# Adaptive layer norm, linear attention and a routed expert layer on one core: weight maxima turned later, norm shifts joined, one turning transfer per tile, filling matmuls in idle stretches

## The chip, the cores and the metric

One Trainium2 chip, of which the kernel uses 1 core. The metric is the time of one execution on the device in microseconds (us). The profile comes from one execution with the hardware profiler on; its span runs from the first to the last recorded instruction.

## What is computed

Input x is 16 batches of 256 tokens with 128 features. A modulation table of shape 16 x 6 x 128, from a small product, gives shifts, scales and gates. Cut to what matters:

```python
h = _layernorm(x) * (1 + ca) + sa
x = x + ga * attention(h)      # relu features, running sums of k v^T, 16 heads of 8
h = _layernorm(x) * (1 + cb) + sb
x = x + gb * ffn(h)
# ffn:
h = rmsnorm(s @ W_in.T, in_norm_w)
logits = h @ Wr.T              # 8 experts, the best 2 of each token, softmax over the two
gate = silu(h @ Wg[e].T); up = h @ Wu[e].T       # 128 -> 512
oe = rmsnorm(gate * up @ Wd[e].T, enorm_w[e])    # 512 -> 128
out = out + gates[:, e:e + 1] * oe
s_hat = rmsnorm(out, out_norm_w) @ W_out.T
```

Everything is fp32 to the outside. The expert weights and the dispatched rows are split in an fp16 high part and an fp16 low part, so that each expert product is three fp16 matmuls.

## The kernel before, in words

All five engines run programs written out by hand, with semaphores between them; nothing schedules. The kernel has three phases.

**Phase one, steps over the 16 batches.** `pipelined` calls `step` on every engine with six stages at once (nrm, qkv, att, prj, inp, rte), each one batch behind the one ahead of it. Steps 0 to 7 are written out, steps 8 to 15 are a hardware loop of two steps a turn, then comes one more step and `drain`, which finishes batches 12 to 15. On TensorE (PE) a step begins with `running_state(att, 0)`: three chunks of three matmuls each against a triangle, into the banks CUM[0] to CUM[2] (L1474). Chunk 0 and 1 come first, then the transposes of the two norms' outputs (L1516, L1525), then chunk 2, which also waits for `den_done`, the denominators of the batch before (VectorE, L1097). There follow the spreading of reciprocals (L1534), keys and values (L1551, L1554), queries (L1561), the output projection (L1578, L1581), `running_state(att, 1)`, the ranks of the chosen experts (L1595 to L1601), the router's input (L1611) and `head_sums` for both halves (L1492 to L1503). VectorE (DVE) makes den and its reciprocal at a step's start, `running_products(att, 0)`, routing and norms, `running_products(att, 1)`, and at the end `weights`. Activations, conversions and the turned copies hT, h2T are on ScalarE (ACT); k v products and the indirect scatters of the routed rows into the table `dispatched` are on GpSimd (POOL): four scatters a batch (L536).

**Weight maxima.** The fp16 split needs one power of two for all expert weights. In steps 3 to 6 `weights` reduces two pieces of the weights each to maxima per partition (L1056), and at the end of step 6 to one column, wmax (L1061, L1062). SCALE_STEP is 7. In that step PE turns wmax to a row (MAX_ROW, in the spare columns of bank CUM[1], L1466) ahead of chunk 1 of the first half, `weight_power` on DVE (L1075 to L1077) takes the power of two, PE broadcasts it to all partitions ahead of chunk 1 of the second half (MAX_ALL, L1469), and `weight_scale` on DVE (L1083 to L1086) makes the factors ahead of `running_products(att, 1)`. From step 8 on the loop converts one eighth of the weights a step.

**Norm shifts.** A norm's shift, minus mean times inverse deviation, is computed by `norm_shift` with one operation for each of the two token tiles of a batch (L883); in the drain the second norm's shift is one operation already (L1220).

**Between the phases.** In the drain PE alternates between `spread` (L1620), `turn` (L1629), `project` (L1636, L1639), `into_experts` (L1651) and `ranks` (L1664 to L1669), each waiting for ACT or DVE. Then PE sums the counts (TOTAL, L1700), DVE computes the tail positions and the table of tiles (39 tiles of 256 rows, each with its expert and first row), SP and ACT write filler rows behind each expert's rows in `dispatched`, and SP waits for all scatters, all fillers and the table, loads the table's first rows to registers (L447), and fetches tile by tile.

**Phase two, tiles.** `load_rows` on SP fetches a tile's high and low rows by two turning (transposing) transfers of 256 rows x 128 fp16 (L433), up to three tiles ahead. PE's `gate_up` runs 24 fp16 matmuls of 256 columns (L1723 to L1725) and `down` 24 of 128 (L1738 to L1740), with the weight's place taken from a register with the expert's number. ACT, DVE and POOL gate, split, weigh and scatter the results. **Phase three** loads the expert rows back, mixes, projects and stores.

## Time and profile before

| what | value |
|---|---|
| median of 3 runs | 413.69 us (413.61 to 415.18) |
| profiled execution, its own time | 414.08 us |
| its span | 412.2 us |
| PE busy | 354.4 us, 86%, 3757 matmuls |
| DVE busy | 323.8 us, 79% |
| ACT busy | 291.9 us, 71% |
| POOL busy | 236.5 us, 57% |
| chain that ended last | PE 70%, DVE 10%, ACT 6%, issue 5%, DMA 4% |
| granted TensorE clock, mean | 0.939 |

The profiled execution's own time is 1.9 us more than its span, which leaves out what lies around the first and last instruction. Phase one ends near 196 us, the tiles run from 209.9 to about 370 us, the rest is phase three. A matmul's shown duration includes the way through the array, so that gapless matmuls overlap in it; the distance of two starts is what one costs. The clock's 1.00 is 2.4 GHz, 0.50 is 1.2 GHz.

### The profile page before, as it was taken

To read this page: it belongs to the slowest core of one execution; us is meant where nothing else is said; L and a number is where in the kernel's file an instruction comes from. 1 tells how busy PE (TensorE), PEld (TensorE's weight loads), DVE (VectorE), ACT (ScalarE), POOL (GpSimd) and SP (SyncE) were. 2 spreads that over 40 slices of the span, in tenths; PEclk is the share of its full clock that TensorE was granted. 3 is DMA by queue.
4 is the path that set the end of the run, shared out by engine and by line. 5 is a ranking of instruction groups with operands and counts; after the bars stand their busy time and mean duration, and the time that the engine had idled before them with its cause. 6 is when DMAs were issued, how large, how long until landed. Compare 5 with 4: busy or idle time off the path is not lost.

```text
span 412.2 us, 12923 instructions
## 1 busy us (share of the span) xinstructions
PE 354.4 (86%) x3757; PEld 307.9 (75%) x3758; DVE 323.8 (79%) x1037; ACT 291.9 (71%) x814; POOL 236.5 (57%) x211
## 2 busy tenths in 40 slices
PE   7899998999999999982069999999999999990464
PEld 4788886888888888861049889989899898980443
DVE  5568998899999999976928887878778877870696
ACT  5465776888888888546328878778778787773595
POOL 0665585688888888856341645454454445453441
PEclk9999998999999999995559999999999999997698
DMA  7899000000000000111423333333333333213833
GB/s 217 356 368 363 2 28 26 8 30 27 26 26 26 26 26 26 34 40 51 131 40 54 68 71 70 62 71 60 64 64 71 60 69 65 57 34 110 351 94 94
DMA packets 46563, 35.68 MB, mean 87 GB/s; under 512 B 36291, under 2 KB 42070, under 8 KB 45750
## 3 DMA queue, kind: packets, MB, share of 16 engines
q1 hardware_dynamic: 41862, 25.40, 21.9%
q0 software_dynamic: 4544, 9.39, 7.0%
q10 hardware_dynamic: 128, 0.53, 0.5%
q8 instruction: 15, 0.25, 0.3%
q14 instruction: 14, 0.11, 0.1%
HBM read 18.69 MB, written 13.47 MB: 78 GB/s over the span
## 4 chain that ended last, share of the span: by engine, by line
PE 70%; DVE 10%; ACT 6%; issue 5%; DMA 4%; POOL 1%; SPq 1%; DVEq 0%; ACTq 0%; POOLq 0%
PE bank L1474 12%; PE bank L1723 9%; PE bank L1724 8%; PE bank L1725 8%; PE bank L1738 4%; PE bank L1740 4%; PE bank L1554 4%; PE bank L1739 4%; PE bank L1497 3%; DVE prod L960 2%; ACT junk L835 2%; DVE wmaxs L1056 1%; PE bank L1561 1%; DMA cst<-consts 1%; PE bank L1581 1%
## 5 line engine op out<-in xcount | busy, mean ns | idle before, releaser
L559 POOL DMA_INDIRECT expert_rows<-late,to_place x78 | 79.2, 1015 | 85.9 <-DVE late L1333 73.3
L1723 PE MATMUL bank<-late,w_hi 128*128 128x256 f16 x312 | 86.4, 277 | 15.1 <-DMA late<-dispatched 13.7
L1724 PE MATMUL bank<-late,w_hi 128*128 128x256 f16 x312 | 86.4, 277 | 0.0
L1725 PE MATMUL bank<-late,w_lo 128*128 128x256 f16 x312 | 86.3, 276 | 0.0
L518 POOL TENSOR_TENSOR kv<-kv,v 128x1024 f32<-128x1024 f32 x32 | 67.7, 2134 | 32.0 <-ACT kv L686 32.0
L1319 DVE SCALAR_TENSOR_TENSOR kv<-bank,uscale,kv 128x512 f32<-128x512 f32 x78 | 58.5, 750 | 30.4 <-ACT kv L777 18.6
L536 POOL DMA_INDIRECT dispatched<-rows,pos x64 | 67.3, 1051 | 25.7 <-issue 18.2
L1474 PE MATMUL bank<-cst,kv 128*128 128x128 f32 x576 | 74.3, 279 | 0.0
L777 ACT ACTIVATE kv<-bank,descale 128x512 f32<-128x512 f32 x78 | 53.6, 687 | 24.0 <-PE bank L1725 20.1
L1474 PEld LDWEIGHTS bank<-cst,kv 128*128 128x128 f32 x576 | 68.9, 193 | 0.3 <-issue 0.2
L783 ACT ACTIVATE kv<-kv 128x512 f16<-128x512 f32 x78 | 48.8, 625 | 16.8 <-DVE kv L1319 12.3
L1326 DVE TENSOR_TENSOR kv<-kv 128x512 f16<-128x512 f32 x78 | 54.4, 697 | 7.5 <-ACT kv L783 5.6
L1738 PE MATMUL bank<-late,kv 128*128 x312 | 54.3, 219 | 0.5 <-DVE kv L1326 0.5
L1739 PE MATMUL bank<-late,kv 128*128 x312 | 54.3, 219 | 0.0
L1740 PE MATMUL bank<-late,kv 128*128 x312 | 54.3, 219 | 0.0
L960 DVE TENSOR_TENSOR prod<-bank,qT 128x384 f32<-128x384 f32 x96 | 49.6, 544 | 0.2 <-issue 0.2
L1723 PEld LDWEIGHTS bank<-late,w_hi 128*128 x312 | 30.9, 99 | 20.5 <-issue 16.5
L1725 PEld LDWEIGHTS bank<-late,w_lo 128*128 x312 | 31.0, 99 | 4.0
L1724 PEld LDWEIGHTS bank<-late,w_hi 128*128 x312 | 31.0, 99 | 3.4
L1738 PEld LDWEIGHTS bank<-late,kv 128*128 128x128 f16 x312 | 30.5, 98 | 1.1 <-issue 0.6
L1739 PEld LDWEIGHTS bank<-late,kv 128*128 128x128 f16 x312 | 30.5, 98 | 0.4
L1740 PEld LDWEIGHTS bank<-late,kv 128*128 128x128 f16 x312 | 30.5, 98 | 0.0
(233 smaller groups left out, 733.2 us busy)
## 6 DMA issues: line engine op xcount, KB each, us to landing
late<-wguT SPq DMA_DIRECT2D x1, 4096.0 KB, 17.8
late<-expert_rows SPq DMA_DIRECT2D x1, 2064.0 KB, 10.9
gates_bc<-gate_rows SPq DMA_DIRECT2D x1, 2048.0 KB, 6.9
wd<-wdT SPq DMA_DIRECT2D x1, 2048.0 KB, 25.0
out<-kv SPq DMA_DIRECT2D x16, 128.0 KB, 1.8
late<-dispatched SPq DMA_TRANSPOSE x78
expert_rows<-late,to_place POOLq DMA_INDIRECT x78
late<-expert_rows SPq DMA_DIRECT2D x1, 1032.0 KB, 6.5
```

Source lines behind the costliest of these rows:

```text
L518: nc.gpsimd.tensor_tensor(kvt[:, 0:HD, :, :], k_in, v_in.to_broadcast([P, HD, H, HD]), ALU.mult).then_inc(kv_done[t], 1)
L536: pool.indirect_dma_start(hbuf, bass.IndirectOffsetOnAxis(ap=pos[:, p, t * K + k:t * K + k + 1], axis=0), rows[:, p, t, k, :], None).then_ ...
L559: pool.indirect_dma_start(ybuf, bass.IndirectOffsetOnAxis(ap=to_place[:, s, r:r + 1], axis=0), yt[:, s, r, :], None).then_inc(y_scat[s], 16)
L960: nc.vector.tensor_tensor(prod[:, t, cc * THIRD * P:(cc + 1) * THIRD * P].rearrange("p (e i) -> p e i", i=P), cum, qT[:, p, t * P:(t + 1) ...
L1319: nc.vector.scalar_tensor_tensor(gu[:, h, :], U[h], uscale[:], sg[:, h, :], ALU.mult, ALU.mult).then_inc(gu_done, 1)
L1474: last = mm(CUM[cc][:, j * P:(j + 1) * P], kv[:, p, t, e * D:(e + 1) * D], tri, start=True, stop=True)
L1723: mm(o, w_hi[:, w], hi, start=True, stop=False)
L1724: mm(o, w_hi[:, w], lo, start=False, stop=False)
L1725: last = mm(o, w_lo[:, w], hi, start=False, stop=True)
L1738: mm(o, gu_hi[:, s % 2, h, g], wd_hi[:, w], start=(f == 0 and r == 0), stop=False)
L1739: mm(o, gu_lo[:, s % 2, h, g], wd_hi[:, w], start=False, stop=False)
L1740: last = mm(o, gu_hi[:, s % 2, h, g], wd_lo[:, w], start=False, stop=(f == FC - 1 and r == RB - 1))
```

## The change

Six edits:

1. The turning of wmax moves from the first half of the scale step to the second (still ahead of chunk 1); the broadcast moves to the step's very end on PE, into spare columns of the bank FFN, behind waits for `wpow_done` and for the chosen slots. On DVE `weight_power` moves behind `running_products(att, 1)` and `weight_scale` to the end of the step, waiting for a new semaphore `wall_ps`.
2. `norm_shift` is one operation for both token tiles.
3. A tile's rows are fetched by one turning transfer of 256 rows x 256 fp16.
4. SP's waits for scatters and fillers move behind the register load.
5. PE's filling matmuls (`keep_busy`, bf16, 512 columns, results unused): 5, 13, 3 and 12 in the drain, 24 behind TOTAL, and 8 once the scatters have landed, ahead of the first tile.
6. The weights' places in the tile phase are formed as byte offsets.

```diff
-        MAX_ALL = CUM[1][:, THIRD * P:THIRD * P + 1]
+        MAX_ALL = FFN[:, L + NT * E:L + NT * E + 1]
...
-            sp.wait_ge(scattered[0], 16 * NT * K * (B // 2))
-            sp.wait_ge(scattered[1], 16 * NT * K * (B // 2))
-            sp.wait_ge(filled, 16 * (E + 1))
             sp.wait_ge(table_done, 1)
...
-                for half in range(2):
-                    sp.dma_start(hT3[:, s, half], hbuf16[bass.ds(row, R), half * D:(half + 1) * D],
-                                 transpose=True).then_inc(slot_ld[s], 16)
+                sp.dma_start(hT3[:, s], hbuf16[bass.ds(row, R), 0:2 * D], transpose=True).then_inc(slot_ld[s], 16)
...
                 sp.load(row_regs, tile_row[0:1, bass.ds(TURN * i, TURN)])
+                if not again_turn(i):
+                    sp.wait_ge(filled, 16 * (E + 1))
+                    sp.wait_ge(scattered[0], 16 * NT * K * (B // 2))
+                    sp.wait_ge(scattered[1], 16 * NT * K * (B // 2))
...
-                for t in range(NT):
-                    last = nc.vector.tensor_scalar(nmr_[:, p, t:t + 1], mv_[:, p, t, 0:1], -1.0, rs_[:, p, t:t + 1],
-                                                   ALU.mult, ALU.mult)
-                last.then_inc(nm_done, 1)
+                nc.vector.scalar_tensor_tensor(nmr_[:, p, :], mv_[:, p, :, 0], -1.0, rs_[:, p, :], ALU.mult,
+                                               ALU.mult).then_inc(nm_done, 1)
...
-                    if scale and cc == 1:
-                        if t == 0:
-                            pe.wait_ge(wmax_done, 1)
-                            mm(MAX_ROW, wmax[:], ident, start=True, stop=True)
-                        else:
-                            pe.wait_ge(wpow_done, 1)
-                            mm(MAX_ALL, ones[0:1, :], wpow_row[:], start=True, stop=True)
+                    if scale and t and cc == 1:
+                        pe.wait_ge(wmax_done, 1)
+                        mm(MAX_ROW, wmax[:], ident, start=True, stop=True)
...
+                if scale:
+
+                    pe.wait_ge(wpow_done, 1)
+                    pe.wait_ge(ohs_done, rte[0] + 1)
+                    mm(MAX_ALL, ones[0:1, :], wpow_row[:], start=True, stop=True).then_inc(wall_ps, 1)
+
+            def keep_busy(bank, n):
+                for _ in range(n):
+                    mm(bank[:].rearrange("p (a n) -> p a n", n=P), ones16[:],
+                       ones16[:].unsqueeze(1).to_broadcast([P, 4, P]), start=True, stop=True)
...
             mm(TOTAL, ones16[:], oh_all[:, B, NT * K, :], start=True, stop=True).then_inc(total_ps, 1)
+            keep_busy(CUM[0], 24)
...
+            def columns_of(w, e, per_expert, at):
+
+                return w.bitcast(U8)[:, bass.ds(e * (2 * per_expert) + 2 * at, 2 * P)].bitcast(F16)
...
             pe.wait_ge(moe_ld, 32)
+            pe.wait_ge(scattered[0], 16 * NT * K * (B // 2))
+            pe.wait_ge(scattered[1], 16 * NT * K * (B // 2))
+            keep_busy(CUM[0], 8)
             turn_of_tiles(0, first=True)
```

PE's program in the scale step, first half, as it stands before (x counts neighbours alike; `bank` is any PSUM bank):

```order
L1503 MATMUL bank<-s,qT 128x16
L1474 MATMUL bank<-cst,kv 128x128 x3
L1466 MATMUL bank<-cst,wmax 1x128
L1474 MATMUL bank<-cst,kv 128x128 x3
L1516 MATMUL bank<-cst,xn 128x128 x2
L1525 MATMUL bank<-cst,xn 128x128 x2
L1474 MATMUL bank<-cst,kv 128x128 x3
L1534 MATMUL bank<-cst,rden 128x128 x2
L1551 MATMUL bank<-bkv,ones 128x512
```

and of the change, the first rows of the step and its second half and end:

```order
L1466 MATMUL bank<-cst,kv 128x128 x6
L1508 MATMUL bank<-cst,xn 128x128 x2
L1517 MATMUL bank<-cst,xn 128x128 x2
L1466 MATMUL bank<-cst,kv 128x128 x3
...
L1466 MATMUL bank<-cst,kv 128x128 x3
L1461 MATMUL bank<-cst,wmax 1x128
L1466 MATMUL bank<-cst,kv 128x128 x6
...
L1495 MATMUL bank<-s,qT 128x16
L1612 MATMUL bank<-wpow_row,cst 128x1
```

The matmul that reads wmax stands behind the projection and chunk 0 of the second half, and the one that reads wpow_row is the last of the step.

DVE's program at the end of the scale step, of the change (before, the three rows of wmax_row and wpow_row stood behind `running_products(att, 0)`, and the four from wpow on ahead of the three `prod`):

```order
L958 TENSOR_TENSOR prod<-bank,qT 128x384 x3
L1073 TENSOR_REDUCE wmax_row<-bank 1x1
L1074 TENSOR_SCALAR wmax_row<-wmax_row 1x1
L1075 TENSOR_SCALAR wpow_row<-wmax_row 1x1
L878 RECIPROCAL rs<-sd 128x2
L998 TENSOR_TENSOR ohs<-oh_all,bank 128x32
L882 SCALAR_TENSOR_TENSOR nmr<-mv,rs 128x2
L1014 TENSOR_REDUCE pos<-ohs 128x4
L1005 TENSOR_REDUCE oh_all<-oh_all 128x8
L1081 COPY wpow<-bank 128x1
L1082 RECIPROCAL wscale<-wpow 128x1
L1083 TENSOR_SCALAR descale<-wpow 128x1
```

The factors' four operations (the fourth, w_by, follows) now stand right ahead of the next step's den.

PE's program at the end of the drain, of the change; before, the same rows stood there without those that read only `ones`:

```order
L1653 MATMUL bank<-small,h2T 128x136 x2
L1616 MATMUL bank<-ones 128x512 x13
L1666 MATMUL bank<-region,ones 128x16
L1668 MATMUL bank<-oh_all,strict 128x16 x2
L1669 MATMUL bank<-oh_all,ones 128x16
L1671 MATMUL bank<-oh_all,ones 128x8 x2
L1631 MATMUL bank<-cst,xn 128x128 x2
L1616 MATMUL bank<-ones 128x512 x3
L1653 MATMUL bank<-small,h2T 128x136 x2
L1616 MATMUL bank<-ones 128x512 x12
```

The fillers stand between `into_experts` and `ranks`, where PE waited for the one-hots, and between `turn` and `into_experts`, where it waited for h2T.

## Rows read from the trace of the kernel before

**Rows 1.** The page's TensorE clock, in 40 slices of the span.

```profile
PEclk9999998999999999995559999999999999997698
```

**Rows 2.** Busy time by stretch; the clock is granted share of 2.4 GHz.

```profile
64.80:68.60 3.80, 1.95 (x16) 1.56 (x16) 3.59 (x11) 1.72 (x6) 2.59 (x3) 1.00 0.11 35
68.70:72.00 3.30, 3.30 (x15) 2.53 (x14) 2.22 (x9) 1.91 (x6) 1.19 (x2) 0.50 0.12 40
181.00:184.70 3.70, 1.85 (x16) 1.34 (x17) 2.88 (x18) 2.78 (x8) 1.24 (x3) 1.00 0.11 36
...
201.30:205.60 4.30, 0.00 (x0) 0.00 (x0) 4.27 (x6) 2.68 (x3) 0.08 (x1) 0.50 0.54 169
...
209.90:215.40 5.50, 5.50 (x27) 3.88 (x28) 0.94 (x2) 1.89 (x3) 1.09 (x1) 0.50 0.27 51
...
390.00:409.90 19.90, 12.95 (x82) 9.72 (x82) 17.41 (x70) 17.01 (x79) 6.76 (x11) 1.00 0.31 90
```

**Rows 3.** PE timeline around the scale step: start, duration, engine, line, operation, idle before.

```profile
57.18 0.39 PE L1551 MATMUL bank<-bkv,ones 3*128 3x512 bf16 x1 [0.20 <-ACT hT L662]
...
64.77 0.92 PE L1474 MATMUL bank<-cst,kv 128*128 128x128 f32 x6
67.54 0.38 PE L1466 MATMUL bank<-cst,wmax 128*1 128x128 f32 x2 [1.85 <-DVE wmax L1062]
...
79.64 1.58 PE L1474 MATMUL bank<-cst,kv 128*128 128x128 f32 x12
```

**Rows 4.** DVE timeline of the same steps and, last row, of the drain.

```profile
54.96 0.18 DVE L1097 TENSOR_SCALAR den<-bank 128x32 f32<-128x32 f32 x1
...
67.50 0.18 DVE L1097 TENSOR_SCALAR den<-bank 128x32 f32<-128x32 f32 x1
...
74.13 0.32 DVE L883 TENSOR_SCALAR nmr<-mv,rs 128x1 f32<-128x1 f32 x2
...
75.92 0.16 DVE L1083 COPY wpow<-bank 128x1 f32<-128x1 f32 x1
...
76.63 1.48 DVE L960 TENSOR_TENSOR prod<-bank,qT 128x384 f32<-128x384 f32 x3
...
181.11 0.16 DVE L1220 SCALAR_TENSOR_TENSOR nmr<-mv,rs 128x2 f32<-128x2 f32 x1
```

**Rows 5.** PE timeline of the drain.

```profile
178.63 0.63 PE L1651 MATMUL bank<-small,h2T 128*128 128x136 f32 x4
...
182.27 0.44 PE L1620 MATMUL bank<-cst,rden 128*128 128x128 f32 x2 [1.44 <-ACT rden L618]
...
184.61 1.01 PE L1651 MATMUL bank<-small,h2T 128*128 128x136 f32 x4
188.55 0.19 PE L1664 MATMUL bank<-region,ones 1*128 1x16 bf16 x1 [2.93 <-DVE oh_all L994]
...
188.94 0.69 PE L1629 MATMUL bank<-cst,xn 128*128 128x128 f32 x2
190.28 1.27 PE L1651 MATMUL bank<-small,h2T 128*128 128x136 f32 x4 [0.66 <-ACT h2T L629]
194.79 0.19 PE L1664 MATMUL bank<-region,ones 1*128 1x16 bf16 x1 [3.24 <-DVE oh_all L994]
```

**Rows 6.** Chain that ended last, from the last scatter on: start, duration.

```profile
200.42 5.17 DMA dispatched<-rows,pos
...
205.66 0.32 SPq L447
...
206.10 1.21 SPq L433
...
207.46 2.28 DMA late<-dispatched
```

**Rows 7.** PE timeline, the first tile matmul.

```profile
209.87 0.39 PE L1723 MATMUL bank<-late,w_hi 128*128 128x256 f16 x1 [13.65 <-DMA late<-dispatched]
```

**Rows 8.** PE timeline, the seven warming matmuls at the kernel's start.

```profile
1.29 3.17 PE L1434 MATMUL bank<-prod 128*128 128x512 bf16 x7 [1.29 <-POOL prod L485]
```

More of the change, by code:

```diff
@@ L21 @@
 U32 = mybir.dt.uint32
+U8 = mybir.dt.uint8
 ALU = mybir.AluOpType
@@ L1072, in weight_power @@
             def weight_power(att):
-                dve.wait_ge(cum_ps[0][1], att[0] + 1)
+                dve.wait_ge(cum_ps[1][1], att[0] + 1)
                 then(nc.vector.tensor_reduce(wmax_row[:], MAX_ROW, AX.X, ALU.max))
@@ L1078, in weight_power, with weight_scale @@
                                         ALU.bitwise_and).then_inc(wpow_done, 1)
-            def weight_scale(att):
-                dve.wait_ge(cum_ps[1][1], att[0] + 1)
+            def weight_scale():
+                dve.wait_ge(wall_ps, 1)
                 then(nc.vector.tensor_copy(wpow[:], MAX_ALL))
@@ L1124, in step @@
                     running_products(att, 0)
-                    if scale:
-                        weight_power(att)
                 if prj is not None:
@@ L1154, in step @@
                 if att is not None:
+                    running_products(att, 1)
                     if scale:
-                        weight_scale(att)
-                    running_products(att, 1)
+                        weight_power(att)
                 if prj is not None:
@@ L1166, in step @@
                     count_chosen(rb, rp)
+                if scale:
+                    weight_scale()
                 if nrm is not None:
@@ L1615, in step @@
                     head_sums(att, 1)
+                if scale:
+                    pe.wait_ge(wpow_done, 1)
[5 more added lines that the diff above has]
+                       ones16[:].unsqueeze(1).to_broadcast([P, 4, P]), start=True, stop=True)
             def spread(b, p, n):
@@ L1685, in drain @@
                 head_sums(b15, 1)
+                pe.wait_ge(cum_used[1][1], B)
+                keep_busy(CUM[1], 5)
                 spread(*b15)
@@ L1690, in drain @@
                 into_experts(*b14)
+                keep_busy(CUM[1], 13)
                 ranks(*b14)
                 turn(*b15)
+                keep_busy(CUM[1], 3)
                 into_experts(*b15)
+                keep_busy(CUM[1], 12)
                 ranks(*b15)
@@ L1720, in gate_up @@
                     o = (G, U)[part][h][:, c * R:(c + 1) * R]
-                    w = bass.ds(e * F + (part * E * F + (h * (FC // 2) + c) * P), P)
-                    mm(o, w_hi[:, w], hi, start=True, stop=False)
-                    mm(o, w_hi[:, w], lo, start=False, stop=False)
-                    last = mm(o, w_lo[:, w], hi, start=False, stop=True)
+                    wh, wl = (columns_of(w[:], e, F, part * E * F + (h * (FC // 2) + c) * P) for w in (w_hi, w_lo))
+                    mm(o, wh, hi, start=True, stop=False)
+                    mm(o, wh, lo, start=False, stop=False)
+                    last = mm(o, wl, hi, start=False, stop=True)
                 last.then_inc((g_ps, u3_ps)[part], 1)
@@ L1734, in down @@
                         pe.wait_ge(gulo_done, 2 * t + h + 1)
-                    w = bass.ds(e * (FC * D) + f * D, D)
+                    wh, wl = (columns_of(w, e, FC * D, f * D) for w in (wd_hi, wd_lo))
                     for r in range(RB):
                         o, g = Y[s % 2][:, r * D:(r + 1) * D], slice(c * R + r * P, c * R + (r + 1) * P)
-                        mm(o, gu_hi[:, s % 2, h, g], wd_hi[:, w], start=(f == 0 and r == 0), stop=False)
-                        mm(o, gu_lo[:, s % 2, h, g], wd_hi[:, w], start=False, stop=False)
-                        last = mm(o, gu_hi[:, s % 2, h, g], wd_lo[:, w], start=False,
+                        mm(o, gu_hi[:, s % 2, h, g], wh, start=(f == 0 and r == 0), stop=False)
+                        mm(o, gu_lo[:, s % 2, h, g], wh, start=False, stop=False)
+                        last = mm(o, gu_hi[:, s % 2, h, g], wl, start=False,
                                   stop=(f == FC - 1 and r == RB - 1))
```

8 lines of the change are left out of this document (3 added, 5 removed).

## The prediction, made blind

> **What bounds it now.** I read the page's clock row first, then the busy shares by stretch, the PE and DVE timelines around the weight maxima, the PE timeline of the drain (the last four batches of phase one, behind the loop), and last the chain that ended last. TensorE is nearly gapless in the steps of phase one and in the tiles of phase two; what can be won lies at three places. The first two show as dips of the granted clock [rows 1].
>
> Place one is the scale step. PE stands idle for 1.85 us ahead of L1466 until DVE has wmax [rows 3], and then works 3.30 us at a granted clock of 0.50 [rows 2]. Place two is the stretch from 184.7 us, in the drain, to 215.5 us, in the first tiles: the clock is at 0.50, PE stands 4.2 to 4.3 us without a matmul before the last scatter lands (from 201.3 us), and the first 27 tile matmuls take 5.50 us [rows 2]. Within it lies place three, the hand-over: last scatter issued at 200.42 and landed 5.17 us later, a register load of 0.32 us, two turning transfers in a row, first matmul at 209.87 [rows 6, 7]. What comes behind 215.5 us I take as shifted as a whole.
>
> **The sum, part by part.**
>
> *1. Maxima moved.* Today the last matmuls that go ahead are the six L1474 from 64.77 us [rows 3]. After the change nothing in the first half waits for wmax. The wait does not vanish: PE's third chunk of running states waits for den (L1097, by den_done), and den stands on DVE behind the same maxima, at 67.50 us [rows 4]. Late next is what hangs on den: reciprocal, its spreading on ACT, then hT on ACT in the same queue. In the step before, den at 54.96 led to PE's L1551 at 57.18, 2.22 us later [rows 3, 4]. So L1551 comes at 67.50 + 2.22 = 69.72. From L1551 to the next step took 57.18 to 64.77, 7.59 us [rows 3]; I add 0.30 for the turning matmul L1466 (0.38 shown, its tail lies under the next one [rows 3]) and the same for the broadcast matmul, now at the step's end: 77.91 against 79.64 [rows 3], 1.73 us won. Then DVE pays: its four chained operations of weight_scale, 75.92 to 76.63 or 0.71 us [rows 4], now stand between the broadcast and den of the next step, whose rden, rrs, ACT's rows and hT all queue behind. PE reaches its own wait for den some 2 us into a step, so part is covered; I price it at 0.45 us, between 0.2 and 0.7. Left: **1.3 us**, if the clock holds. It may: ahead of the fall PE now stands 1.85 us in one piece [rows 3], afterwards some 1.1 us ahead of the third chunk (two chunks and four transposes behind 64.77 it gets there at 66.6) and 0.6 us ahead of the spreading transposes, and the tail runs at clock 1.00 with PE busy 12.95 of 19.90 us [rows 2]. If it falls, nothing is left of this term. Bounds 0 and 1.8.
>
> *2. Norm shifts.* Two operations of 0.16 us each (0.32 together) become one like L1220 of 0.16 [rows 4]. There are two such pairs a step, so DVE gets back some 0.2 to 0.3 us a step, but PE is the full engine; only in the steps with the maxima, where DVE is late, does it count, once or twice 0.1. **0.2 us**, bounds 0 and 0.8.
>
> *3. Filling in the drain.* 5, 13, 3 and 12 filling matmuls of 512 columns. Seven like them at the start took 3.17 us, the last's tail among it, so 0.42 apart [rows 8], which is 512 columns at 1.2 GHz; at 2.4 GHz half, 0.21. The gaps they stand in are 1.44, 2.93, 0.66 and 3.24 us [rows 5]; they fill 1.05, 2.75, 0.65 and 2.55 of them at the upper clock, so they fit, the second with least to spare since its gap shortens too. What they give: the second and third L1651 groups took 1.01 and 1.27 us where one at full clock took 0.63, and the transposes L1629 0.69 where some 0.4 is the full-clock time [rows 5]. That is 0.38 + 0.64 + 0.3 = **1.3 us** on the chain PE, ACT, DVE, positions, scatter. The scatters of the batch before occupy POOL to about 195.1, so of the last batch's start at 196.65 about 1.25 can be won. Bounds: 1.3 won, 5 us lost (rival C).
>
> *4. Hand-over.* The register load moves ahead of the wait: **0.35 us** [rows 6]. Two transfers of 256 rows x 256 bytes become one of 256 x 512. Today's second starts at 207.46 and lands 2.28 later; the issue alone is 1.21 [rows 6]. A merged one can cost from one issue (lands 1.36 us earlier than now) to both (lands as now), and no row shows which. I take the middle, nearer to both, since SP's issue time looks like work per row: **0.6 us**, bounds 0 and 1.36, below nothing only if the wider form is slower. The trace puts 1.21 us of issue on 64 KB. The Trainium skill (DMA: Bandwidth & Descriptors, Rules for kernel authors) says of small transfers to coalesce, since under 64 KB one pays mostly overhead; by that rule the full 1.36 would be won, and the sum would be 0.7 us larger.
>
> *5. Filling before the tiles.* 24 more after the totals take 24 x 0.21 = 5.1 us and end when the tables do, so they delay nobody. PE then waits for the scatters, idle for 4.2 us as now [rows 2], and issues 8 more once they have landed. That idleness most likely takes the clock down again (it fell behind 1.85 us in the scale step), so the 8 cost 3.4 us, not 1.7. The scatter lands 1.25 us sooner, at 204.35; the fill ends at 207.85. The turned tile lands at 205.60 - 1.25 + 0.1, and 3.64 (206.10 to 209.74) less 0.6, so at 207.5: PE starts tile 0 at about 207.9 instead of 209.87 [rows 7]. So 1.97 us of earlier start, in place of 1.25 + 0.35 + 0.6 = 2.2: the fill eats 0.2 to 0.4. But the activity that lifts the clock now begins at 204.4. Before it took 215.5 - 209.9 = 5.6 us from first matmul to full clock; from 204.4 on that is 210.0 at the latest, so 2.1 us of tiles at half rate at most, about 1.3 as I take it, instead of 5.5. Half of the difference of 4.2 is **2.1 us** won; bounds 1 and 2.8.
>
> *6. Register form.* Offsets in bytes change one register operation per weight group on PE's sequencer; the tile matmuls run at a steady pitch, so the sequencer is covered. Nothing; 0.3 either way. In the tiles the transfer is issued three tiles ahead, so its form costs nothing unless one issue took over 3 us: SP now spends 2 x 1.21 of about 4 us a tile.
>
> Sum: 1.3 + 0.2 + 1.97 + 2.1 = 5.6 us. The profiled execution took 414.08 us (span 412.2), 0.39 above the median of 413.69, so the forecast is 414.08 - 5.6 - 0.39 = 408.1; for the fill's delay, which I may have low, I say **408.3 us**.
>
> **Rivals.**
> A. *The clock doesn't follow.* It falls in the scale step and comes back late in the tiles: terms 1 and 5 shrink to 0 and 1. Sum 0.2 + 1.97 + 1.0 = 3.2, time 410.5. For it: it fell in the scale step at 68.7 us although PE had worked 1.95 of the 3.80 us before [rows 2], and the idle is not all gone. Against: a block of gapless matmuls stands ahead of the tiles. Chance 0.2.
> B. *Covered or replaced.* The wait for den and the delayed weight_scale eat all of term 1, the merged transfer costs two issues, and the 8 fillers stand in front of a tile already landed. Left about 1.5 us of clock: 412.2. Chance 0.1.
> C. *Slower.* The fillers themselves run at half rate in the drain: 13 x 0.42 = 5.5 us in a gap of 2.93, 12 x 0.42 = 5.0 in 3.24, and the 24 then take 10 us where 5.2 are free. Each comes before ranks, on which positions and scatters wait. First tile at 209.87 + 2.6 + 1.8 + about 3, cold start saved: 414.08 + 7.4 - 1.5 - 2.8 - 0.39 = 416.8. It decides from a pitch of 2.93 / 13 = 0.23 us on. For it: the clock was at 0.50 from 184.7 on, and PE had worked but 1.85 of the 3.70 us before [rows 2]. Against: the first five fall in just that stretch. Chance 0.04; another 0.02 for a merged transfer over 3 us that would make SP the bound.
> D. *More than summed.* One issue for the transfer and full clock throughout: the 8 fillers end before the tile lands at 206.7, a start 1.2 us earlier, and term 5 is 2.75: 408.1 - 1.2 - 0.65 = 406.3. Chance 0.14, and the forecast's own case has 0.5.
>
> **How the numbers follow.** A measurement here can tell 0.5%, 2.07 us, from no change: faster means below 411.6. The forecast case with its term bounds spans 406.6 to 410; with A and D the range is 405.8 to 411.2. Faster 0.84, same 0.10, slower 0.06.
>
> **What would show it.** No idle before the turning matmul, but about 1 us idle before the third chunk of the scale step, and step 8 begun near 78 us. L1651 groups of about 0.63 us in the drain, no gap there left; last scatter issued near 199.2. First transfer 0.1 us behind the landing; its issue between 1.2 and 2.4 us. First tile near 206.4 (207.9 less the 1.5 of terms 1 and 2), full clock within 2 us of it. Wrong would be: fillers 0.42 us apart in the drain, DVE's weight_scale holding up PE by over 1 us in step 8, or tiles waiting for transfers.

## The result and the profile after

The change makes the kernel slower: 434.91 us median of 4 runs (429.68 to 438.62) against 414.44 (413.61 to 416.49, 4 runs) on the same chip, a ratio of 1.038 with a 95% interval of 1.030 to 1.046. Two of the four executions, of 438.29 and 438.62 us, fell in a slower state, with a mean granted clock of 0.92 where the other two show 0.94 and 0.96, and the ratio leaves them out. The forecast was 408.3 us, range 405.8 to 411.2. The profiled execution took 431.53 us, its span is 429.6, against 412.2 before: 17.4 us more.

The page of the changed kernel, the busy times and TensorE's clock (answers to [rows 1]):

```profile
PE 375.1 (87%) x3822; PEld 319.4 (74%) x3823; DVE 342.2 (80%) x1007; ACT 292.5 (68%) x814; POOL 239.0 (56%) x211
...
PEclk8599998899999999999998999999999999996597
```

DVE has 18.4 us more work (342.2 against 323.8) from a change that gives it fewer instructions. One line holds it. The joined shift: durations of its 32 instructions in ns (least, median, greatest), and below them who waited for it (us, times):

```profile
L882 DVE SCALAR_TENSOR_TENSOR nmr<-mv,rs x32: 141/161/2093, 6.1 to 209.2; 128x2 f32<-128x2 f32 x32
...
  ACT xn L601: 22.4, 15
```

and the same answer for the one-column form of the kernel before:

```profile
L883 DVE TENSOR_SCALAR nmr<-mv,rs x60: 193/205/216, 6.1 to 171.0; 128x1 f32<-128x1 f32 x60
...
  ACT xn L601: 2.9, 2
```

The median of the joined form is what the prediction took, 0.16 us; its maximum is 13 times that, and the mean is 0.90 us. Where the long ones lie shows in the timeline of one loop step of the changed kernel, all engines (start, duration, engine, line; the idle time before in brackets):

```profile
171.88 0.37 PE L1495 MATMUL bank<-s,qT 128*128 128x16 f32 x2
...
177.56 4.22 POOL L518 TENSOR_TENSOR kv<-kv,v 128x1024 f32<-128x1024 f32 x2 [0.32 <-ACT kv L686]
...
177.66 2.05 DVE L882 SCALAR_TENSOR_TENSOR nmr<-mv,rs 128x2 f32<-128x2 f32 x1
...
179.63 0.18 DVE L992 TENSOR_TENSOR oh_all<-bank,i 128x32 f32 x1
...
179.84 0.88 ACT L601 ACTIVATE xn<-x_all,nmr,rs 128x128 f32 x2 [1.46 <-DVE nmr L882]
...
180.24 0.16 PE L1587 MATMUL bank<-region,ones 1*128 1x16 bf16 x1 [0.85 <-DVE oh_all L992]
...
182.59 0.43 PE L1484 MATMUL bank<-qT,s 128*32 128x128 f32 x8 [0.54 <-DVE prod L958]
...
183.85 0.37 PE L1495 MATMUL bank<-s,qT 128*128 128x16 f32 x2
```

GpSimd's k v product, two instructions of 2.13 us, begins at 177.56. The shift is issued 0.10 us later and ends at 179.71, with the first of the two products (177.56 + 2.13 = 179.69). Behind it on DVE everything is 1.7 us later than behind the two operations of 0.32 us together: the one-hots, for which PE waits 0.85 us, and the products, for which it waits 0.54 us more. ACT waits 1.46 us with its xn. Of the 32 shifts 15 are held up, and each of these ends 0.01 to 0.03 us behind the GpSimd product that it was issued into. The same place before:

```profile
89.76 0.37 PE L1503 MATMUL bank<-s,qT 128*128 128x16 f32 x2
...
95.44 4.23 POOL L518 TENSOR_TENSOR kv<-kv,v 128x1024 f32<-128x1024 f32 x2 [0.32 <-ACT kv L686]
...
95.54 0.32 DVE L883 TENSOR_SCALAR nmr<-mv,rs 128x1 f32<-128x1 f32 x2
...
100.04 0.37 PE L1503 MATMUL bank<-s,qT 128*128 128x16 f32 x2
```

The same instruction of GpSimd at the same distance, and the one-column forms run through it. They are not alone in that; two more operations that start inside a product, in the kernel before:

```profile
95.78 0.18 DVE L994 TENSOR_TENSOR oh_all<-bank,i 128x32 f32 x1
...
98.56 0.15 DVE L878 RECIPROCAL rs<-sd 128x2 f32<-128x2 f32 x1
```

A TENSOR_TENSOR with one of its two inputs in a PSUM bank, and a reciprocal of two columns: neither is held up. A step is the distance of two last head-sum matmuls (L1503, now L1495): 10.28 us before, 11.97 after, 1.69 more. By stretch (columns as in [rows 2]: PE, PEld, DVE, ACT, POOL busy, clock, DMA share, GB/s), the loop step before,

```profile
98.94:109.22 10.28, 10.20 (x114) 8.83 (x110) 9.74 (x45) 8.29 (x25) 8.78 (x7) 1.00 0.08 26
```

and of the changed kernel a loop step, the drain's fillers, the idle stretch ahead of the last landing, the 8 fillers, the first 27 tile matmuls, and the tail, at the place that corresponds to 390.00 to 409.90 in [rows 2]:

```profile
171.88:183.85 11.97, 10.58 (x113) 9.04 (x112) 11.32 (x42) 8.38 (x24) 8.81 (x7) 1.00 0.07 22
202.70:216.00 13.30, 11.67 (x72) 5.96 (x71) 9.94 (x59) 9.35 (x30) 8.48 (x10) 1.00 0.14 45
222.20:225.60 3.40, 0.00 (x0) 0.00 (x0) 3.40 (x3) 2.37 (x3) 0.00 (x0) 1.00 0.51 190
225.60:229.20 3.60, 3.30 (x8) 1.19 (x9) 1.33 (x2) 0.00 (x0) 2.12 (x1) 0.53 0.27 59
229.30:232.00 2.70, 2.70 (x27) 2.42 (x26) 0.75 (x1) 1.26 (x2) 2.29 (x1) 1.00 1.25 62
406.50:426.40 19.90, 15.02 (x82) 12.32 (x80) 16.37 (x67) 17.17 (x78) 6.56 (x11) 0.82 0.30 86
```

Before, PE was the full engine of a step (10.20 of 10.28). Afterwards DVE is (11.32 of 11.97), and PE has 1.4 us of gaps. The whole account, in the span: the last step ends at 202.64 us instead of 180.56, 22.1 us later. From there to the first tile 26.6 us instead of 29.3, tiles 157.7 instead of 160.65, the tail 42.6 instead of 41.6. 22.1 - 2.7 - 2.95 + 0.95 = 17.4 us. So gains of the size that the prediction summed are there, and an edit that it priced at 0.2 us gives back more than three times as much. Not all of the 22.1 us is the shifts': 3.0 us are already there at the first head sums (26.66 us against 23.65), and some 2 of these come from TensorE's rate at the very start, which differs between executions (experiment 6). The seven steps inside the loop add 11.7 us, the written-out steps 4 to 6 another 7.0: 11.13, 13.61 and 13.92 us instead of 9.93, 10.60 and 11.11. The 0.95 us of the tail go with a granted clock of 0.82 where the kernel before had 1.00 [rows 2].

The drain and the hand-over of the changed kernel, PE timeline (answers to [rows 5] and [rows 7]), and in the last row SP's issues of the first three turning transfers:

```profile
207.15 2.97 PE L1616 MATMUL bank<-ones 128*128 128x512 bf16 x13
...
211.73 0.73 PE L1653 MATMUL bank<-small,h2T 128*128 128x136 f32 x4
212.30 2.75 PE L1616 MATMUL bank<-ones 128*128 128x512 bf16 x12
215.38 0.18 PE L1666 MATMUL bank<-region,ones 1*128 1x16 bf16 x1 [0.33 <-DVE oh_all L992]
...
216.65 5.34 PE L1616 MATMUL bank<-ones 128*128 128x512 bf16 x24
225.90 3.53 PE L1616 MATMUL bank<-ones 128*128 128x512 bf16 x8 [3.91 <-DMA dispatched<-rows,pos]
229.26 0.27 PE L1735 MATMUL bank<-late,w_hi 128*128 128x256 f16 x1
...
225.95 3.96 SPq L430 DMA_TRANSPOSE late<-dispatched  x3
```

and its chain, where the last scatter lands (answers to [rows 6]):

```profile
221.01 4.76 DMA dispatched<-rows,pos
225.76 0.14 issue
225.90 3.53 PE bank L1616 x8
```

The fillers run at the upper level, 0.21 us apart; the last eight, behind 3.9 us of idleness, at the lower one, 0.42 apart; the first 27 tile matmuls take 2.7 us where they took 5.50 [rows 2].

### The profile page after: what moved, and what is told of

It is laid out like the page before. It is cut to its first block, busy times and chain, and to the rows that moved or that the text cites. A ratio compares the mean times of both kernels' runs of the same rounds, so it can differ in the third digit from the quotient of the medians.

```text
span 429.6 us, 12945 instructions
## 1 busy us (share of the span) xinstructions
PE 375.1 (87%) x3822; PEld 319.4 (74%) x3823; DVE 342.2 (80%) x1007; ACT 292.5 (68%) x814; POOL 239.0 (56%) x211
## 4 chain that ended last, share of the span: by engine, by line
PE 51%; DVE 25%; issue 12%; ACT 4%; DMA 4%; POOL 2%; DVEq 1%; SPq 0%; ACTq 0%; POOLq 0%
PE bank L1735 8%; PE bank L1737 8%; PE bank L1736 8%; DVE prod L958 6%; PE bank L1466 4%; PE bank L1750 4%; PE bank L1752 4%; PE bank L1751 4%; DVE nmr L882 2%; PE bank L1546 2%; DVE st L866 2%; DVE rows L1019 1%; POOL dispatched L536 1%; DMA cst<-consts 1%; DVE prod L1377 1%
## 5 line engine op out<-in xcount | busy, mean ns | idle before, releaser
L559 POOL DMA_INDIRECT expert_rows<-late,to_place x78 | 81.3, 1043 | 79.7 <-DVE late L1329 67.1
L1735 PE MATMUL bank<-late,w_hi 128*128 128x256 f16 x312 | 85.1, 273 | 1.2 <-issue 0.9
L1736 PE MATMUL bank<-late,w_hi 128*128 128x256 f16 x312 | 85.0, 273 | 0.0
L1737 PE MATMUL bank<-late,w_lo 128*128 128x256 f16 x312 | 85.0, 273 | 0.0
L1466 PE MATMUL bank<-cst,kv 128*128 128x128 f32 x576 | 76.3, 284 | 1.2 <-DVE den L1095 1.2
L1466 PEld LDWEIGHTS bank<-cst,kv 128*128 128x128 f32 x576 | 70.9, 198 | 2.1 <-issue 2.0
L601 ACT ACTIVATE xn<-x_all,nmr,rs 128x128 f32<-128x128 f32 (+1 forms) x64 | 28.0, 484 | 22.4 <-DVE nmr L882 22.4
L1750 PEld LDWEIGHTS bank<-late,kv 128*128 128x128 f16 x312 | 30.5, 98 | 1.0 <-issue 0.6
L1751 PEld LDWEIGHTS bank<-late,kv 128*128 128x128 f16 x312 | 30.5, 98 | 0.4
## 6 DMA issues: line engine op xcount, KB each, us to landing
late<-expert_rows SPq DMA_DIRECT2D x1, 2064.0 KB, 11.1
```

What stands on the lines that cost most here:

```text
L559: pool.indirect_dma_start(ybuf, bass.IndirectOffsetOnAxis(ap=to_place[:, s, r:r + 1], axis=0), yt[:, s, r, :], None).then_inc(y_scat[s], 16)
L1466: last = mm(CUM[cc][:, j * P:(j + 1) * P], kv[:, p, t, e * D:(e + 1) * D], tri, start=True, stop=True)
L1735: mm(o, wh, hi, start=True, stop=False)
L1736: mm(o, wh, lo, start=False, stop=False)
L1737: last = mm(o, wl, hi, start=False, stop=True)
L1750: mm(o, gu_hi[:, s % 2, h, g], wh, start=(f == 0 and r == 0), stop=False)
```

## Experiments

**Theory.** The joined shift reads two operands from SBUF (the on-chip memory in which all operands but those in PSUM banks lie) and is held up by GpSimd's k v product, which reads SBUF too, until that instruction ends. The Trainium skill (SBUF — State Buffer, Who interferes with whom) says that a VectorE instruction with two SBUF inputs contends with a GpSimd instruction that reads SBUF, not with one that only writes it, that whichever is issued first has the shared ports for its whole length and the other is fully blocked, and that tensor_scalar contends as well where it enters a mode that reads through two ports. The trace agrees: issued 0.10 us behind a 2.13 us product, the shift takes 2.05 us. The rivals: an added delay anywhere on DVE's chain is amplified; the two norms' shifts both matter; or the loss comes from another edit. Chips differ: the kernel before took 431.28 us on the chip of e1 to e4, 415.07 on that of f1 to f4, 431.15 on that of h1 and h4, and 414.94 on that of j1 to j4. So each ratio is to the kernel before on the same chip.

**1. The change with two shift operations again** (e1, then f1 and j4 on other chips).

```diff
-                nc.vector.scalar_tensor_tensor(nmr_[:, p, :], mv_[:, p, :, 0], -1.0, rs_[:, p, :], ALU.mult,
-                                               ALU.mult).then_inc(nm_done, 1)
+                for t in range(NT):
+                    last = nc.vector.tensor_scalar(nmr_[:, p, t:t + 1], mv_[:, p, t, 0:1], -1.0, rs_[:, p, t:t + 1],
+                                                   ALU.mult, ALU.mult)
+                last.then_inc(nm_done, 1)
```

> The changed kernel with norm_shift back to two operations; everything else stays changed. Theory (the joined operation reads two SBUF tensors and waits for the k v product L518 on GpSimd, about 2 us in every step): phase one returns to steps of 10.28 us instead of 11.97, the start of the drain comes some 20 to 22 us sooner, the time is 407 to 411 us. Rival (the later turning of the maxima or the fillers slow the steps): the steps stay near 12 us and the time at 430 us.

> The version with two operations again, on one chip with the versions that each lack one more part, as their measure: 5 to 9 us faster than before.

> The change with two shift operations, again, as partner of the run without the later maxima: 0.984 to 0.988 of the kernel before on the same chip.

Measured: ratios 0.985 (0.979 to 0.991), 0.987 (0.981 to 0.992) and 0.989 (0.985 to 0.993). This one edit turns 3.8% slower into 1.1 to 1.5% faster. 1.35% of 415.07 us is 5.6 us, the size of the prediction's sum; f1's ratio rests on four of its six executions, and the medians of all give 0.991. On the slower chips the gain is another one: the kernel before, traced on the chip of h1 (h3, 432.31 us), spends 169.0 us in the tiles and h1 159.9, while from the last step's end to the last scatter's issue e1 takes 24.0 us and h3 23.9. So e1 and h1 show what the joined shift costs, but they do not bear out the prediction's other terms.

**2. The joined shift alone on the kernel before** (e2).

```diff
-                for t in range(NT):
-                    last = nc.vector.tensor_scalar(nmr_[:, p, t:t + 1], mv_[:, p, t, 0:1], -1.0, rs_[:, p, t:t + 1],
-                                                   ALU.mult, ALU.mult)
-                last.then_inc(nm_done, 1)
+                nc.vector.scalar_tensor_tensor(nmr_[:, p, :], mv_[:, p, :, 0], -1.0, rs_[:, p, :], ALU.mult,
+                                               ALU.mult).then_inc(nm_done, 1)
```

> The kernel before with nothing but the joined norm shift. Theory: L518 is waited for in every step, steps of about 12 us, the time 434 to 438 us, that is 20 to 23 us above before. Rival (the joined operation is cheap, as 0.16 us in the drain says, and the loss needs the other edits): within 2 us of before, 412 to 415 us.

Measured: 1.051 (1.045 to 1.057). The loss needs nothing else of the change.

**3. Which of the two, and does the order decide?** In e3 only the second norm's shift is joined (`if nmr_ is nmr:` the two operations, else the one). In h1 only the first norm's is joined, and it stands directly behind its reciprocal, ahead of the search for the chosen experts' indices, so that it is issued before the product instead of behind it.

```diff
                     norm_inv(nb, sd, rs, ln_sd, ln_rs, np_)
+                    norm_shift(nb, mv, rs, nmr, ln_rs, ln_nm, np_)
                 if rte is not None:
                     best_index(rb, rp)
-                if nrm is not None and not (isinstance(nb, int) and nb < 2):
-                    norm_shift(nb, mv, rs, nmr, ln_rs, ln_nm, np_)
```

> The changed kernel with two operations for the first norm's shift and the joined one for the second norm's. Theory: in steps of 10.28 us the second shift falls in the last 0.9 us of the second L518 (before: 98.75 against an end at 99.68), so it takes up to 0.9 us instead of 0.33, most of it in the slack that VectorE has ahead of den: 0 to 6 us above the version with two operations everywhere. Rival (only the first shift's place matters, the second is short as in the changed kernel's trace, 0.16 us): within 1 us of it, or 0.5 us faster.

> The changed kernel with two operations for the second norm's shift and the joined one for the first norm's, placed directly behind the reciprocal, ahead of the index search, some 0.45 us earlier. Theory: it starts before the first L518 does (0.1 us behind k_done) in most steps and then lasts 0.16 us; the steps are 10.3 to 10.5 us, the time within 2 us of the version with two operations. Where it comes later than the start of L518 it waits the full 2.1 us. Rival: its place changes nothing, 2 us each, steps near 12 us.

Measured: e3 0.987 (0.979 to 0.996), h1 0.988 (0.979 to 0.997), two ratios that lie within the interval of two operations (e1, 0.979 to 0.991, on e3's chip). The moved joined shift of h1 and its place:

```profile
L888 DVE SCALAR_TENSOR_TENSOR nmr<-mv,rs x16: 160/161/2086, 6.1 to 163.8; 128x2 f32<-128x2 f32 x16
```

```profile
153.35 0.16 DVE L888 SCALAR_TENSOR_TENSOR nmr<-mv,rs 128x2 f32<-128x2 f32 x1
...
153.54 4.23 POOL L518 TENSOR_TENSOR kv<-kv,v 128x1024 f32<-128x1024 f32 x2 [0.34 <-issue]
```

The same instruction, 0.19 us ahead of the product instead of 0.10 behind it, takes 0.16 us; two of the sixteen still catch a product (0.96 and 2.09 us). So the loss in the loop is the first shift's, and it is an accident of 0.3 us in the order of issue. In e3 the second shift waits too (median 0.69 us, up to 1.55). In the loop that costs 0.1 us a step (10.6 us on average, e1 10.5), but not in the written-out steps: step 4 takes 11.1 us in the changed kernel, in e2 and in e3, all of which join the second shift, and 9.9 in h1 and e1, which do not; step 5 takes 13.6, 13.6 and 13.3 against 10.6. So some 4 of the 22.1 us are the second shift's, and the rival that both matter holds there. The medians, with intervals of 0.9% either way, cannot show 4 us.

**4. An unread operation ahead of the shifts of the kernel before.** Its two columns come from two inputs in e4, from one in h4, and j1 has one column of one input. One of the three marked lines stands in each run.

```diff
+                if nmr_ is nmr:
+                    nc.vector.tensor_tensor(spare_nm[:], mv_[:, p, :, 0], rs_[:, p, :], ALU.mult)            # e4
+                    nc.vector.tensor_scalar(spare_nm[:], rs_[:, p, :], -1.0, None, ALU.mult)                # h4
+                    nc.vector.tensor_scalar(spare_nm[:, 0:1], rs_[:, p, 0:1], -1.0, None, ALU.mult)          # j1
```

> The kernel before with one more, unused operation ahead of the first norm's two shifts: a tensor_tensor product of 2 columns, of another operation kind than the joined shift but with both inputs in SBUF. Theory (two SBUF inputs are what waits for GpSimd): it lasts 1 to 2 us whenever L518 runs, steps near 12 us, 430 to 438 us. Rival (the wait belongs to scalar_tensor_tensor or to the strided mean): 0.16 us each, 413 to 416 us.

> The kernel before with one more, unused tensor_scalar of 2 columns ahead of the first norm's two shifts (one SBUF tensor, no second). Theory: 0.16 us each, it does not wait for GpSimd, within 1.5 us of before. Rival (one more VectorE operation in that place costs as such, since VectorE is nearly full): 10 us or more.

> The kernel before with one more operation a step that nobody reads: a TENSOR_SCALAR of one column, one input, ahead of the two shift operations of the first norm, in the place where the runs with an unused two-column operation lost 21 to 24 us. If only forms that need a second read from SBUF (two inputs, or an even number of columns read two at a time) wait for GpSimd's k v product, the one-column form costs its own 0.06 to 0.1 us a step: 0 to +1.5 us, ratio 1.000 to 1.004, mean about 150 to 200 ns. If any added operation at this place delays VectorE's chain, +15 to +25 us as with the two-column forms.

Measured: e4 1.056 (1.047 to 1.065), h4 1.045 (1.036 to 1.053), j1 1.002 (0.9995 to 1.004). The durations of the unread operation, of e4,

```profile
L884 DVE TENSOR_TENSOR spare_nm<-mv,rs x16: 141/1778/2087, 6.1 to 186.2; 128x2 f32<-128x2 f32 x16
```

of h4,

```profile
L884 DVE TENSOR_SCALAR spare_nm<-rs x16: 149/1144/2084, 6.2 to 182.4; 128x2 f32<-128x2 f32 x16
```

and of j1, whose unread operation starts inside a k v product in 11 of the 16 cases, of which the timeline shows one:

```profile
L884 DVE TENSOR_SCALAR spare_nm<-rs x16: 132/134/154, 6.1 to 161.9; 128x1 f32<-128x1 f32 x16
```

```profile
99.99 4.23 POOL L519 TENSOR_TENSOR kv<-kv,v 128x1024 f32<-128x1024 f32 x2 [0.32 <-ACT kv L687]
...
100.09 0.13 DVE L884 TENSOR_SCALAR spare_nm<-rs 128x1 f32<-128x1 f32 x1
```

h4 was a miss: I had expected a form with one input not to wait. It does, with two columns, and with one it does not, though it starts 0.10 us into the product just as well. The rival that any added operation at this place costs as much falls with j1. The Trainium skill (VectorE: DVE Perf Modes, What auto-detection actually checks) says that an operation with one source runs in a two-port mode where source and destination lie in SBUF and their outermost dimensions, those of length 1 not counted, are both even or equal. The Trainium skill (SBUF — State Buffer, Who interferes with whom) counts that mode as contending. h4's two columns agree with it; j1's single column has no dimension to test, and there the measured 0.13 us decides: it doesn't wait. No run here shows the mode itself.

**5. GpSimd writing instead of reading** (j2, the kernel before with the joined shift).

```diff
-                        nc.gpsimd.tensor_tensor(kvt[:, 0:HD, :, :], k_in, v_in.to_broadcast([P, HD, H, HD]),
-                                                ALU.mult).then_inc(kv_done[t], 1)
+                        nc.gpsimd.tensor_tensor(kvt[:, 0, 0, 0:2], v[:, p, t, 0:2], v[:, p, t, 2:4], ALU.mult)
+                        kf = kv[:, p, t, 0:HD * D]
+                        nc.gpsimd.memset(kf[:, 2:HD * D], 0.0).then_inc(kv_done[t], 1)
```

> The kernel before with the joined shift, and GpSimd's k v product replaced by a multiplication of two columns (which carries the wait) and a memset of the other 1022 columns; the k v product is left out, so the output and the routing are not the reference's, and only the shift's own duration is read. If the shift waits for GpSimd's reads of SBUF alone, none of the 32 shifts waits, mean 160 to 200 ns. If it waits for any GpSimd instruction that touches SBUF, those that start under a memset end with it, and the mean lies well above 400 ns.

Measured, one execution: 416.17 us beside 414.94 for the kernel before. The median of its 30 shifts is 0.16 us and the greatest 0.67. GpSimd's part is shorter here, 0.94 us instead of 2.13, so the time alone proves little. The timeline has both cases:

```profile
33.22 1.28 POOL L528 TENSOR_TENSOR gates_bc<-gates_bc,small 128x512 f32<-128x512 f32 x1
...
33.87 0.65 DVE L883 SCALAR_TENSOR_TENSOR nmr<-mv,rs 128x2 f32<-128x2 f32 x1
...
87.76 0.94 POOL L520 MEMSET kv<- 128x1022 f32 x1
...
87.96 0.16 DVE L883 SCALAR_TENSOR_TENSOR nmr<-mv,rs 128x2 f32<-128x2 f32 x1
```

Issued into another product that reads SBUF (33.22 to 34.50) the shift ends with it, at 34.52, one of three such cases; so the expectation that none of the shifts waits overlooked these products. Issued into a memset it takes 0.16 us. That case is there only once, since in the other steps the shift is issued just ahead of the memset. That writes alone do not block it rests on this one instance; the Trainium skill's rule above says the same.

**6. What the other edits are worth**, each on the version with two shifts or on the kernel before.

f2: two shifts, no `keep_busy` anywhere.

```diff
-                keep_busy(CUM[1], 13)
...
-            keep_busy(CUM[0], 24)
...
-            keep_busy(CUM[0], 8)
```

> Two operations, and all 65 filling matmuls left out (drain, behind the totals, ahead of the tiles). Theory of the prediction: the drain is back at 1.2 GHz from about 185 us on (1.3 us longer) and the first tiles are half speed for about 5 us instead of 0 to 2 (2 us longer), while a fill no longer stands ahead of a landed tile: 3 to 4 us slower than the version with the fillers. Rival (what fills stands in the way as much as it helps): within 1 us of it.

f3: the kernel before with the later weight maxima alone, and j3, below, the same undone on the version with two shifts.

```diff
-                    if scale and cc == 1:
-                        if t == 0:
-                            pe.wait_ge(wmax_done, 1)
-                            mm(MAX_ROW, wmax[:], ident, start=True, stop=True)
-                        else:
-                            pe.wait_ge(wpow_done, 1)
-                            mm(MAX_ALL, ones[0:1, :], wpow_row[:], start=True, stop=True)
+                    if scale and t and cc == 1:
+                        pe.wait_ge(wmax_done, 1)
+                        mm(MAX_ROW, wmax[:], ident, start=True, stop=True)
...
                     running_products(att, 1)
+                    if scale:
+                        weight_power(att)
```

> Before, with nothing but the later turning of the maxima. Prediction: 1.3 us won, between 0 and 1.8 (scale step 2 us shorter, the step behind it up to 0.7 longer, clock at 1.00 if it holds). Rival (the wait moves to den and the chained operations of weight_scale, now ahead of den, hold up the next step): 0 to 1 us slower than before.

> The change with two shift operations and with the weight maxima turned where they were before; fillers, register load and single transfer stay. If the later maxima win their 1.3 us (prediction's term 1, and 1.3 us shorter steps 7 and 8 in the traces), this is 1.3 us slower than the version with them, ratio to the kernel before 0.989 to 0.991. If they win nothing in time, as the run with the maxima alone said, both stand within 0.3%, about 0.9865.

f4: two shifts, two turning transfers a tile.

```diff
-                sp.dma_start(hT3[:, s], hbuf16[bass.ds(row, R), 0:2 * D], transpose=True).then_inc(slot_ld[s], 16)
+                for half in range(2):
+                    sp.dma_start(hT3[:, s, half], hbuf16[bass.ds(row, R), half * D:(half + 1) * D],
+                                 transpose=True).then_inc(slot_ld[s], 16)
```

> Two operations, all fillers, but two turning transfers a tile. The changed kernel's trace shows one merged issue at 1.20 us, like one of the two before. Theory: the first tile lands 1.3 us later, of which the 8 fillers ahead of it hide most: 0 to 1.3 us slower than with one transfer. Rival (merged transfers also free DMA engines and SP in the tile phase): 2 us or more slower.

| run | edit | ratio to the kernel before | interval |
|---|---|---|---|
| f1 | two shifts | 0.9865 | 0.981 to 0.992 |
| f2 | f1 without fillers | 0.9979 | 0.9955 to 1.0003 |
| f4 | f1 with two transfers | 0.9955 | 0.993 to 0.998 |
| f3 | before with later maxima | 1.0022 | 0.9999 to 1.0045 |
| j4 | two shifts, other chip | 0.9888 | 0.985 to 0.993 |
| j3 | j4 without later maxima | 0.9872 | 0.984 to 0.990 |

Against f1 the fillers are worth 1.1%, 4.7 us, by intervals that don't touch, and the single transfer 0.9%, 3.7 us, by intervals that just don't touch. Together that is 8.4 us of a gain of 5.6, so the second is likely too large: f4's interval meets j4's, and between their traces f1 is ahead of f4 by 0.6 us from the last step to the first tile and by 1.25 us in the tiles, 1.8 in all. Between f1 and f2 it is 1.9 and 2.2 us. The later maxima are worth nothing that can be measured, in either pair, although the traces show the steps shorter. The ends of step 5 and of step 8, in f3, and of step 5 in the kernel before, whose step 8 ends at 89.76 (above):

```profile
55.33 0.38 PE L1499 MATMUL bank<-s,qT 128*128 128x16 f32 x2
...
90.33 0.37 PE L1499 MATMUL bank<-s,qT 128*128 128x16 f32 x2
```

```profile
53.44 0.37 PE L1503 MATMUL bank<-s,qT 128*128 128x16 f32 x2
```

35.00 us to 90.33 against 36.32 from 53.44 to 89.76, 1.3 us less, the size of the term. But f3's profiled execution entered the stretch 1.9 us later, since its matmuls at the very start (L1550, the keys) still ran at half rate there: 2.07 us for four at 16.34 where the kernel before shows 1.13 at 16.05. So spans of single executions differ by about 2 us from the start alone, in programs that are the same there. And the gain is not there in every execution. The same four matmuls in f2's scale step, which has the later maxima too:

```profile
72.96 2.04 PE L1550 MATMUL bank<-small,hT 128*128 128x256 f32 x4
```

In f1 they take 1.13 us there. In f2 the granted clock fell all the same (0.59 from 74 to 77 us), behind gaps of PE of 1.04 and 0.34 us that f1 has as well, and its two steps take 14.31 + 11.24 = 25.55 us, no less than the 25.21 before. How often that happens is not known, so what eats the 1.3 us in the medians is left open.

f4 shows where a second transfer hurts. SP's queue and PE at the second tile:

```profile
202.59 8.52 SPq L431 DMA_TRANSPOSE late<-dispatched  x6
...
210.19 0.28 PE L1741 MATMUL bank<-late,w_hi 128*128 128x256 f16 x1 [0.95 <-DMA late<-dispatched]
```

Six issues take 8.52 us where three of double width take 3.96 in the changed kernel: an issue of 256 rows costs 1.2 us whether 128 or 256 elements wide. With two per tile the second tile comes 0.95 us late. In the kernel before the first tile's matmuls at half rate, 5.50 us [rows 2], may have given that transfer the time; that is argued, not tried.

No run is faster than the version with two shifts beyond its interval, nor does it need to lose edit 2 altogether: h1 and e3 stand beside it within their intervals. The version to keep is the change with the two one-column shifts.

## Why the prediction was wrong

**Term 2, the norm shifts, failed, and it alone.** It said that two operations of 0.16 us "become one like L1220 of 0.16 [rows 4]", 0.2 us won, bounds 0 and 0.8. The price was a row of the drain, at 181.11, where no k v product runs any more; the last product of the kernel before is issued at 169.7. At the place of the edit GpSimd works on a product from 0.1 us before the shift on. The lower bound of 0 excluded a loss for no reason but that fewer instructions are less work. Measured: 11 of the 16 first shifts and 4 of the 16 second ones wait, up to 2.09 us, mean of all 32 0.90 us. Phase one ends 22.1 us later, and, the start's 2 us or so apart, that is the joined shifts' work: e2 loses as much without any other edit. The overlap could be read before the run, in the timelines of DVE and POOL at 95.44 and 95.54 shown above, and the rule that makes an overlap a wait stood in the Trainium skill (SBUF — State Buffer, Who interferes with whom), on which the prediction did not draw. The term also argued that DVE's time doesn't count since PE is the full engine. DVE was idle for 10.28 - 9.74 = 0.54 us of a step; that idle time covered next to nothing, since 1.7 us more on DVE at this place made the step 1.69 us longer.

No rival covered it: C, the slower one, needed fillers over 0.23 us apart in the drain, and they ran at 0.21 at a clock of 1.00.

**Term 1, maxima moved: mechanism right, gain not in the time.** With two shifts both steps together take 23.88 us (12.64 + 11.24, f1) instead of 25.21 (14.87 + 10.34), 1.3 us as summed, and the clock held at 1.00 in that stretch of f1. That the sum fits is luck: the scale step won 2.2 us and not 1.73, and the step behind it lost 0.9 us to the delayed factors, for which I had taken 0.45 and at most 0.7. Both pairs of runs (f3, and j4 against j3) come out 0.2% slower with the later maxima, neither clear of 0, and in f2 the clock fell there, as rival A had it. So the term belongs at 0 until shown otherwise. In the changed kernel itself DVE is late through the waits, and the two steps take 12.59 + 12.86 us.

**Term 3, filling in the drain: right.** 13 fillers took 2.97 us, 12 took 2.75, and the L1653 groups 0.63 and 0.73 us where the two took 1.01 and 1.27 [rows 5]. From the last step's end to the last scatter's issue it took 19.86 us before, and in f1 18.68: 1.2 us won of the 1.3. f2, without fillers, has the idle gaps of 2.93 and 3.24 us back, and takes 20.57 us.

**Term 4, hand-over: right mechanism, somewhat small.** From the issue of the merged transfer to its landing f2's chain shows 2.74 us, where the first issue of the two to the second landing was 3.64 [rows 6]: 0.9 us, for which I took 0.6 between 0 and 1.36. And where the prediction gave the transfer nothing in the tiles, f4 lost 0.95 us at the second. By the Trainium skill (DMA: Bandwidth & Descriptors, Rules for kernel authors), which says to coalesce small transfers, I had weighed 1.36; the measured 0.9 us lies between.

**Term 5, filling before the tiles: right.** From landing to first tile 3.5 us (225.77 to 229.26) instead of 4.28; the clock did fall, the eight fillers ran 0.42 apart and ended last, so they cost what was said, 0.4 us against f2's 3.04. The tiles took 157.7 instead of 160.65 us, 2.95 where 2.1 was forecast with a bound of 2.8; the first 27 of their matmuls, at least, ran at a clock of 1.00. But f2 and f3, without fillers, are 0.7 us shorter in the tiles than the kernel before, so the fillers' own part is about 2.2 us.

**Term 6, register form: nothing**, as far as the tile matmuls' steady pitch of 0.11 us shows.

So a sum of 5.6 us met 4.6 to 6.3 us in three measurements of the kernel without the joined shift, in part by luck. Between the traces of the kernel before and of f1, the start costs 2.1 us, the steps win 1.3, last step to first tile 2.96, the tiles 2.96, and the tail costs 0.5. Of the first 2.96 us, 1.0 are the last scatter's way, 4.19 us instead of 5.17, which no term had and which varies (4.76 in the changed kernel, 4.61 in f2). The forecast for the kernel as it is missed by 26.6 us (23.2 for the profiled execution), for the smallest term that it gave a size.

## What to carry to other kernels

Before two small VectorE operations are made one, look at how many operands the new form reads from SBUF and what GpSimd does at the moment of its issue. Here one column with the second operand as a scalar slipped past a GpSimd product; two inputs from SBUF, or a TENSOR_SCALAR of two columns, waited for its end. Take the price of an operation from the place where it will stand, beside the neighbours it will have there, not from the same form in a quiet stretch; and give an edit on a nearly full engine (DVE 95% busy in a loop step here) a lower bound below zero. Where such a form is wanted all the same, issue it ahead of GpSimd's instruction: 0.3 us earlier made 2.05 us into 0.16.

## What the hardware showed that I had not expected

- A VectorE operation on two columns waits for a GpSimd product of 2.13 us to its end, both with two inputs from SBUF (up to 2.09 us) and as a TENSOR_SCALAR with one (up to 2.08). A TENSOR_SCALAR of one column takes 0.13 us at the same place, and a reciprocal of two columns inside a product 0.15.
- One operation of 0.16 us a step, issued 0.10 us behind a GpSimd product instead of 0.19 ahead of it, costs the kernel most of 5.1% (e2), through the waits of ACT and PE.
- The issue of a turning transfer of 256 rows takes 1.2 us at 128 and at 256 elements.
- At the kernel's start the rate of the matmuls differs between executions of the same code (four matmuls 1.13 or 2.07 us) with the granted clock at 1.00 in both (the kernel before and f3, from 16 us on; in the changed kernel it reads 0.50 there), so that row does not tell all there.
- Over 3.4 us without a matmul the granted clock reads 1.00 and 0.53 on the fillers behind it (the stretches from 222.20 and 225.60): the fall is to be read from what follows, not from the idle stretch.
